# Expert stage of a layer: where the expert weights are buffered, when they are loaded, and how the stage begins

## The reference

```
gu  = buf[e] @ w_gate_up[e]        # [tokens, 512] @ [512, 512]
act = silu(gu[:, :256]) * gu[:, 256:]
y   = act @ w_down[e]              # [tokens, 256] @ [256, 512]
out[token] += weight[token, e] * y
```

## Time and profile before

| | us |
|---|---|
| median of 3 runs | 1019.9 (1015.76 to 1022.46) |
| the profiled execution, time | 1025.01 |
| the profiled execution, span | 1023.2 |
| TensorE busy / VectorE / ScalarE / GpSimd | 905.2 / 771.3 / 503.7 / 495.9 |

### The profile page before, as it was taken

The page is one execution under the profiler, slowest core; times in us unless marked ns, Lnnn a source line. Parts: engine busy times, 40 slices in busy tenths (PEclk is TensorE's granted clock), DMA queues, the critical chain, the costliest instruction groups (busy, mean ns, idle before and its releaser), DMA issues. The chain is left out here.

```text
span 1023.2 us, 14443 instructions
## 1 busy us (share of the span) xinstructions
PE 905.2 (88%) x4313; PEld 731.7 (72%) x4313; DVE 771.3 (75%) x1837; ACT 503.7 (49%) x867; POOL 495.9 (48%) x420
## 2 busy tenths in 40 slices
PE   5789999999999999999699999999379897687960
PEld 3577888888888888888488888888357575566740
DVE  6978888888888888888777777776768767485720
ACT  5455555555555554555642333332258766475730
POOL 2456676666667666666400000000065566656652
PEclk9989999999999999999999999999679989797985
DMA  8001111111111111103755654431189979798743
GB/s 295 6 32 47 57 41 53 47 57 42 58 47 57 37 58 47 56 33 104 264 171 184 254 184 146 145 105 54 44 287 280 321 218 283 212 276 235 184 61 41
DMA packets 52758, 131.01 MB, mean 128 GB/s; under 512 B 12156, under 2 KB 14588, under 8 KB 46528
## 3 DMA queue, kind: packets, MB, share of 16 engines
q1 hardware_dynamic: 41248, 114.67, 32.4%
q0 software_dynamic: 11424, 15.29, 8.6%
HBM read 106.53 MB, written 35.91 MB: 139 GB/s over the span
## 5 line engine op out<-in xcount | busy, mean ns | idle before, releaser
L595 POOL TENSOR_TENSOR a_t<-a_t 128x512 f32<-128x512 f32 x80 | 105.2, 1315 | 101.7 <-DVE a_t L358 101.7
L1081 DVE TENSOR_TENSOR w_l<-raw,w_h 128x1024 fp32r<-128x1024 f32 x96 | 114.7, 1222 | 13.5 <-ACT w_h L1074 13.2
L604 POOL TENSOR_TENSOR a_fQ<-a_fQ,a_den 128x512 f32<-128x512 f32 x64 | 88.0, 1376 | 71.8 <-DVE a_den L396 71.8
L213 PE MATMUL a_PQ<-w_h,a_xT_h 128*128 128x512 f32 x384 | 107.8, 403 | 10.0 <-DVE w_l L345 9.3
L775 PE MATMUL r_PY<-w_h,r_o_h 128*128 128x512 f32 x256 | 106.3, 415 | 3.4 <-DVE r_o_l L867 3.4
L1179 POOL DMA_INDIRECT out<-m_y,si x38 | 66.2, 1741 | 88.0 <-DMA out<-m_y,si 64.5
L1051 POOL TENSOR_SCALAR r_vr<-r_mv 128x1 f32<-128x1 f32 x16 | 8.4, 526 | 199.0 <-DVE r_mv L878 199.0
L213 PE MATMUL a_PQ<-w_l,a_xT_h 128*128 128x512 f32 x384 | 104.2, 394 | 0.0
L213 PE MATMUL a_PQ<-w_h,a_xT_l 128*128 128x512 f32 x384 | 103.5, 392 | 0.0
L775 PE MATMUL r_PY<-w_l,r_o_h 128*128 128x512 f32 x256 | 101.9, 398 | 0.0
L775 PE MATMUL r_PY<-w_h,r_o_l 128*128 128x512 f32 x256 | 101.8, 398 | 0.0
(11 more groups left out here) (168 smaller groups left out, 2193.8 us busy)
## 6 DMA issues: line engine op xcount, KB each, us to landing
raw<-in_wgu SPq DMA_DIRECT2D x32, 1024.0 KB, 6.8
oT<-a_o SPq DMA_DIRECT2D x64, 256.0 KB, 2.5
raw<-in_wd SPq DMA_DIRECT2D x32, 512.0 KB, 6.4
v_l<-oT SPq DMA_DIRECT2D x11, 1024.0 KB, 6.6
v_h<-oT SPq DMA_DIRECT2D x5, 1024.0 KB, 6.7
out<-r_x SPq DMA_DIRECT2D x18, 256.0 KB, 2.0
a_xin<-in_x SPq DMA_DIRECT2D x16, 256.0 KB, 3.2
v_l<-in_wq SPq DMA_DIRECT2D x4, 1024.0 KB, 12.4
```

The lines of the kernel that those rows point to most:

```text
L213: last = eng.matmul(bank[:, :], a[:, k, :], w[:, 4 * i + k, :], start=s == 0 and k == 0, stop=s == 2 and k == 3)
L595: eng.tensor_tensor(t1[:, r % 2, :], t1[:, r % 2, :], t2[:, r % 2, :], ALU.add).then_inc(sm["xr"], 1)
L604: eng.tensor_tensor(q, q, den[:, n % 2, :].unsqueeze(2).broadcast_to([P, 4, P]), ALU.mult).then_inc(sm["fs"], 1)
L1081: eng.tensor_tensor(low, src, high.bitcast(F32), ALU.subtract).then_inc(sm["m_wl"], 1)
```

## The change

- The raw weights get 8 buffers of 1.5 MiB, a `ring`, instead of 3. Three lie where `raw` lay. Four lie in the space of `w_l`, which holds `Wo` until the last output projection. The eighth is made of a free corner of `w_h` and of space in the expert block. The low parts no longer have a place of their own: VectorE writes them over the raw weights.
- Loads issued by routing: experts 0, 1 and 2 as before, the up weights of 7 in chunk 5; behind the last projection, ahead of the last store of the token weights, experts 3 and 4; behind that store expert 5. Loads issued by the expert block: 6 and the down weights of 7 behind the first gathers, and `e+8` once GpSimd has issued the scatter of `e` (semaphore `m_sent`).
- The weights lie in DRAM as `[expert, 4, 128, 512]`, and a load reads 4 (or 2) pieces of 2 KB for each partition.
- The `spare` DMA and `no_scatter` go. All scatters count on one semaphore, and the only scatter of a one-tile expert counts twice.
- TensorE, VectorE and ScalarE get the first two rounds written out: `down(0)` comes ahead of `up(1)`. VectorE clears all six gather buffers first. ScalarE waits for `ident` after the first two splits instead of before.

```diff
+                    if c == 5:
+                        load_up(sm, eng, ring, wgu, 7)
                 for t in range(2):
                     eng.dma_start(out[T + t * P:T + (t + 1) * P, :], x2[:, 1, :]).then_inc(sm["r_so1"], 16)
+                eng.wait_ge(sm["r_y"], NC)
+                for e in (3, 4):
+                    load_up(sm, eng, ring, wgu, e)
+                    load_down(sm, eng, ring, wd, e)
                 store_w(NC - 1)
+                load_up(sm, eng, ring, wgu, 5)
+                load_down(sm, eng, ring, wd, 5)
...
+RING = 8
+
+def load_up(sm, eng, ring, wgu, e):
+    up, _, _, _ = ring[e % RING]
+    eng.dma_start(up, wgu[e].rearrange("k p f -> p k f")).then_inc(sm[f"m_wg{e % RING}"], 16)
...
-                for e in range(3, NE):
-                    eng.wait_ge(sm["m_wl"], 3 * (e - 3) + 2)
-                    eng.dma_start(raw[e % 3][:, 0:4, :], wgu[e]).then_inc(sm[f"m_wg{e % 3}"], 16)
-                    eng.wait_ge(sm["m_wl"], 3 * (e - 3) + 3)
-                    eng.dma_start(raw[e % 3][:, 4:6, :], wd[e]).then_inc(sm[f"m_wd{e % 3}"], 16)
+                load_up(sm, eng, ring, wgu, 6)
+                load_down(sm, eng, ring, wd, 6)
+                eng.wait_ge(sm["m_g11"], 16)
+                load_down(sm, eng, ring, wd, 7)
+                for e in range(RING, NE):
+                    eng.wait_ge(sm["m_sent"], e - RING + 1)
+                    load_up(sm, eng, ring, wgu, e)
+                    load_down(sm, eng, ring, wd, e)
+                eng.wait_ge(sm["m_s"], 32 * NE)
...
                 for e in range(NE):
-                    no_scatter(e)
                     if e + 6 < NE:
                         gather(e + 6, 0)
                         gather(e + 6, 1)
-                    scatter(e, 0)
+                    load_flag(eng, regs, e)
                     with eng.If_lt(regs[e % 7], T):
-                        scatter(e, 1)
+                        scatter(e, 0, 16)
+                        scatter(e, 1, 16)
+                        eng.sem_inc(sm["m_sent"], 1)
+                    with eng.Else():
+                        scatter(e, 0, 32)
+                        eng.sem_inc(sm["m_sent"], 1)
...
                 load_flag(eng, regs, 0)
                 both(eng, regs, 0, turn, "m_xt1")
-                for e in range(NE + 1):
+                load_flag(eng, regs, 1)
+                both(eng, regs, 0, up, "m_gu1")
+                both(eng, regs, 1, turn, "m_xt1")
+                both(eng, regs, 0, turn_a, "m_at1")
+                load_flag(eng, regs, 2)
+                both(eng, regs, 2, turn, "m_xt1")
+                both(eng, regs, 0, down, "m_yd1")
+                both(eng, regs, 1, up, "m_gu1")
+                for e in range(2, NE + 1):
...
-                clear(0)
-                clear(1)
+                for i in range(6):
+                    clear(i)
                 w_low(1, (0, 1))
...
-                    if e >= 4:
-                        eng.wait_ge(sm["m_s0" if t == 0 else f"m_s1{e % 2}"], 16 * (e - 3 if t == 0 else e // 2 - 1))
+                        eng.wait_ge(sm["m_s"], 32 * (e - 3))
...
-        "wgu": np.asarray(L0_ffn_w_gate_up).reshape(NE, 4, P, 512).transpose(0, 2, 1, 3),
+        "wgu": np.asarray(L0_ffn_w_gate_up).reshape(NE, 4, P, 512),
```

More of the change, by code:

```diff
@@ L1101, in experts @@
         y = sb("y", [P, 4, 2, D])
-        spare = sb("spare", [1, 2, 16])
+        with nc.sbuf_tensor("m_raw", [P, 2, 512], F32) as raw:
+            pass
+        low = sb("low", [P, 2, 512], F32R)
         ident = sb("ident", [P, P])
@@ L1108, in experts @@
         PY = [ps("PY0"), ps("PY1")]
+        ring = ring + [(v_h[:, 20:24, :], raw[:, :, :], w_h[:, 20:24, :], low[:, :, :])]
         def f(ap):
@@ L1163, in gather, with scatter @@
                         bounds_check=T - 1, oob_is_err=False).then_inc(sm[f"m_g{t}{e % 6}"], 16)
[L1165 to L1173, removed]
+                def scatter(e, t, done):
                     i = 2 * e + t
                     if t == 0 and e >= 1:
-                        eng.wait_ge(sm["m_s0"], 16 * e)
-                        eng.wait_ge(sm[f"m_s1{(e - 1) % 2}"], 16 * ((e + 1) // 2))
+                        eng.wait_ge(sm["m_s"], 32 * e)
                     eng.wait_ge(sm[f"m_y{t}"], e + 1)
@@ L1289, in _ @@
                 both(eng, regs, 0, x_low, "m_xTl1")
-                for i in range(2, 6):
-                    clear(i)
                 w_low(1, (2,))
-                for e in range(NE + 1):
+                load_flag(eng, regs, 1)
+                both(eng, regs, 0, act, "m_a1")
+                both(eng, regs, 1, x_low, "m_xTl1")
+                both(eng, regs, 0, a_low, "m_al1")
+                w_low(2, (0, 1, 2))
+                load_flag(eng, regs, 2)
+                both(eng, regs, 2, x_low, "m_xTl1")
+                both(eng, regs, 1, act, "m_a1")
+                w_low(3, (0, 1, 2))
+                for e in range(2, NE + 1):
                     load_flag(eng, regs, e + 1)
@@ L1349, in _ @@
                 w_high(1, (2,))
-                for e in range(NE + 1):
+                load_flag(eng, regs, 1)
+                both(eng, regs, 0, silu, "m_si1")
+                both(eng, regs, 1, x_high, "m_xTh1")
+                both(eng, regs, 0, a_high, "m_ah1")
+                w_high(2, (0, 1, 2))
+                load_flag(eng, regs, 2)
+                both(eng, regs, 2, x_high, "m_xTh1")
+                both(eng, regs, 0, weigh, "m_y1")
+                both(eng, regs, 1, silu, "m_si1")
+                w_high(3, (0, 1, 2))
+                for e in range(2, NE + 1):
                     load_flag(eng, regs, e + 1)
@@ L1372, in build @@
         si = ctx.enter_context(nc.sbuf_tensor("si", [P, 64], U32))
-        raw = [ctx.enter_context(nc.sbuf_tensor(f"raw{i}", [P, 6, 512], F32)) for i in range(3)]
-        routing(nc, sm, x, wo, wc, bias, cr, oT, xn2d, out, gi, si, raw, wgu, wd, w_h, w_l, v_h, v_l)
-        experts(nc, sm, wgu, wd, xn2d, out, gi, si, raw, cr, w_h, w_l)
+        with nc.sbuf_tensor("raw", [P, 18, 512], F32) as raw:
+            pass
+        low = ctx.enter_context(nc.sbuf_tensor("low", [P, 18, 512], F32R))
+        ring = [(v[:, i:i + 4, :], v[:, i + 4:i + 6, :], w[:, i:i + 4, :], w[:, i + 4:i + 6, :])
+                for v, w, n in ((raw, low, 3), (v_l, w_l, 4)) for i in range(0, 6 * n, 6)]
+        ring7 = ring + [(v_h[:, 20:24, :], None, None, None)]
+        routing(nc, sm, x, wo, wc, bias, cr, oT, xn2d, out, gi, si, ring7, wgu, wd, w_h, w_l, v_h, v_l)
+        experts(nc, sm, wgu, wd, xn2d, out, gi, si, ring, cr, w_h, w_l, v_h)
 def kernel(L0_attn_x, L0_attn_Wq, L0_attn_Wk, L0_attn_Wv, L0_attn_Wo, L0_ffn_w_cls, L0_ffn_bias,
```

74 lines of the change are left out of this document (38 added, 36 removed).

## The result

The changed kernel takes 1040.6 us in the median of 4 runs (1035.8 to 1044.6), the kernel before 1018.8 on the same chip. The ratio is 1.021, interval 1.015 to 1.027. The prediction was 986 with a range from 967 to 1012: wrong in its sign. By the medians 21.8 us were lost. The profiled executions show half of that: the one after (1035.8 us) is the quickest of its four and has a span of 1033.9, the one before (1025.0) lies above its median and has 1023.2.

A forecast was written before the change was run, and what follows sets the result against it. It took the serial chain of scatters, slowed by landings on full DMA engines, to bound the kernel. Terms: -3 - 1 - 32.8 + 2.5 = -34, profiled 1025.0 to 991, 986 us on the median's scale; range 967 to 1012.

The forecast's parts named there:

- Loads behind scatters: SyncE issues the load of e+8 once scatter e is out; priced at 0, up to +6 us.
- rival B: Scatter landing does not change, period stays 8.0 to 8.2 us, only the beginning wins: 1012 to 1016 us; chance 0.13.
- The sum's main term: Between the scatters of experts 2 and 24, 22 periods fall from 8.19 to 6.7 us: -32.8 us.
- DMA demand of 6.9 us: Per period, one expert's weights (4.4 us) and q0's tiles (2.5 us) need 6.9 us of all DMA engines.
- The chain's lag: At the end, the last scatter was to start within 8 us of the last copy to `y`, not 17.
- Loads moved ahead: Experts 3, 4, 5 and up weights of 7 move 16.2 us of engine time into 725 to 745; cost 0 to +4.
- rival D: Early loads delay the store and first gather by as much as they save: 1002 us; chance 0.15 shared with period 7.1 to 7.8.
- Pieces of 2 KB: In weight loads, 2 KB pieces cost 4 us but may shorten a scatter's landing from 9.1 to about 6 us.
- Rival C: 2 KB pieces lose their turns beside scatters; dearer q1 eats the gain from 3.6 us per MB, 1034 at 4.0; chance 0.07.
- The other rule weighed there: DMA engines turn between queues by packets of 9 to 17 descriptors; could leave landing unshortened and period near 8 us.
- The spare DMA and the counting: Removing 26 x (1.16 + 0.3) us from GpSimd's list, beside a scatter's landing; priced at 0.
- The beginning: Down 0 ahead of up 1 and earlier clears move scatter 0 from 768.41 to about 765.5: -3 us, bounds -6 and +1.

The follow-up runs named there:

- e5_tiny: The changed kernel with loads of experts 8 to 31 shrunk to 128 bytes per partition, results not the reference's: 968.8 us in one run.
- e1_marked: The changed kernel with the signal m_sent put on a GpSimd memset behind the scatter: 979.1 us, ratio to before 0.962.
- e6_marked8k: e1_marked with pieces of 8 KB for up and 4 KB for down weights: 995.0 us, ratio to before 0.977.
- e7_noearly: e1_marked with experts 3, 4, 5 and the up weights of 7 loaded in the expert block: 987.4 us, ratio to before 0.970.
- e3_pieces8k: The changed kernel with the weight layout of before, pieces of 8 KB and 4 KB: 1023.4 us, ratio to before 1.005.
- e10_before2k: The kernel before with 2 KB weight pieces alone: 1013.6 us, ratio to before 0.995.
- e8_dose: The changed kernel with down weights loaded at once and up weights only behind a memset after the scatter: 1009.6 us, ratio 0.990.

## Why the prediction was wrong

**The diagnosis was right.** The chain of scatters bounds the kernel, at 8.19 us a period where TensorE needs 5.5, and the landing on busy engines makes it so. e5_tiny shows it directly: without the bytes the period is 6.07. It shows too that 5.5 was too low: in that run TensorE is busy for 173.4 of 180 us.

**The step that failed is "Loads behind scatters".** I wrote that "SyncE issues `e+8` when scatter `e` is out" and priced it at 0, up to +6. I asked only whether the load would be late for its split. I did not ask what the signal certifies. It is raised before the scatter's row begins, and the load goes 0.2 us ahead. Measured, the period is 9.06 instead of 6.7: 2.36 x 22 = 52 us, and by the medians e1_marked gets 61.5 us back by moving the signal. Even rival B ("the landing does not change") was too kind, because no case had a landing that gets worse by being synchronized. A sign of it was there: behind the scatter at 841.49 show 9.1 us, and SyncE's queue, which I did not read beside it, has a load issued 0.1 us ahead. I took an average of 8.19 for the cost of load; the single distances of one-tile experts ran from 5.6 to 11.9.

**The sum's main term was right for the kernel that I thought I was reading.** e1_marked has a period of 6.73 against 6.7 forecast, DMA at 0.98 from 765 to 900 and 979.1 us against 986. The other terms are off: 21.1 us to scatter 0 for 24.8, 21.7 for 20, 39.1 from scatter 24 to the last for 44, 9.0 behind it for 12.3. And there is luck in the 6.7. It was taken from a DMA demand of 6.9 us, and e6_marked8k has a period of 6.60 with DMA only 0.89 busy, so that this demand sets the period is not shown. The chain's lag did not go either: the last scatter starts 14.6 us behind the last copy to `y`, where the forecast had under 8. (A slip that changes nothing: 4 us for 39.9 MB are 0.16 for an expert's 1.57 MB, not 0.13.)

**Loads moved ahead:** the mechanism holds. DMA is 0.85 busy from 725 to 745 and the block begins 0.2 us earlier (740.4; without the early loads, in e7_noearly, at 740.7), so rival D falls. The size was 16.2 us; e7_noearly measures 8.3, and only once the order is right.

**Pieces of 2 KB:** I took +4 us for their price and a landing of 6 for their help. In the changed kernel they cost 17 us (e3_pieces8k), and alone in the kernel before they win half a per cent (e10_before2k). The landing is short because the scatter is first, not because pieces are short: 6.60 with 8 KB, 6.73 with 2 KB. Rival C pointed at a dearer q1. From 745 to 1034 in the changed kernel:

```profile
q1 hardware_dynamic: 20272, 39.85, 44.0%
q0 software_dynamic: 10461, 14.96, 27.1%
```

That is 0.440 x 289 / 39.85 = 3.19 us per MB, below the 3.6 from which C decides. The same stretch in e3_pieces8k, e1_marked and e6_marked8k:

```profile
q1 hardware_dynamic: 7344, 39.85, 40.7%
q1 hardware_dynamic: 20272, 39.85, 38.4%
q1 hardware_dynamic: 7344, 39.85, 34.3%
```

These are 2.95, 2.79 and 2.49. So both raise the price: the wrong order by 0.40 to 0.46 us per MB, pieces of 2 KB against 8 KB by 0.24 to 0.30, more than the 0.21 that I had as the most. With the order right the dearer bytes did not lengthen the period. The other rule weighed there, packets of several descriptors by which an engine turns between its queues (the Trainium skill, DMA: Bandwidth & Descriptors, "Queues, rings and completion order"), would keep the landing unchanged by piece length if a packet held all pieces of a partition. With the order right, the periods of 6.60 and 6.73 agree with it; the packets are not shown by any run, and with the wrong order the period does depend on the pieces (8.50 and 9.06).

**The spare DMA and the counting:** priced at 0, they or the new end of the block gave 3.1 us. From the last scatter to the end all kernels with the old list have 12.3 us and all with the new one 8.9 to 9.4. Which edit does it was not separated.

**The beginning:** -3 forecast with bounds -6 and +1, -5.1 measured at scatter 0.

## What to carry to other kernels

A signal that follows a DMA in an engine's list need not mean that the transfer is ahead of what the signal releases: here it came 0.2 us before the scatter's row. When two queues share the DMA engines, let an instruction that the same engine executes behind the DMA carry the signal (here a memset on GpSimd), and check in the timeline which of the two was issued first.

When a latency on a serial chain varies, don't average it: set its instances beside all transfers issued around them, not the nearest alone. Gating one transfer by another fixes their phase for every round, at a good value or at a bad one.

## What the runs showed of the hardware

With no load beside it, a scatter of 128 rows of 2 KB was followed by the next, which waits for its landing, after 4.8 to 5.1 us (kernel before, experts 26 and 28 to 30), and its packets flowed from 2.2 to 4.4 us after its start. With a load of 1.5 MiB issued 0.2 us ahead, the packets began at about 5 us, and in the window from 822 to 827 the scatter's queue got 2.6% of the engines and the load's 84.9%: the load, issued first, was served nearly alone. Whether the scatter's descriptors lay ready in that time or reached the engines late is not shown. With the load 1.8 us behind the scatter's start, the scatter's queue had 51.3% from 821 to 824. A third of the bytes ahead gave half of the delay in time, and 0.42 of it by the period (e8_dose).
